# Joint attention with values as weights: four heads' exponentials as one streamed operand, normalised on GpSimd

## What is computed

```
kv_in = concatenate([context_hidden, draft_hidden], axis=1)
k, v = kv_in @ Wk.T, kv_in @ Wv.T          # 4 heads each, repeated for 4 query heads
scores = einsum('bhqd,bhkd->bhqk', q, k) * SCALE
probs = softmax(scores, axis=-1)
attn = einsum('bhqk,bhkd->bhqd', probs, v)
return attn @ Wo.T                          # added to x, then the next layer norm
```

## Time and profile before

| | us |
|---|---|
| three runs | 2807.26, 2809.73, 2812.78 (median 2809.73) |
| profiled execution, span from first to last instruction | 2808.8 |
| stage `joint4` within it | about 1883 to 2275 |

### The profile page before, as it was taken

One profiled execution on the slowest core, in us unless ns is written; L12 is line 12 of the kernel. 1 busy time (PEld: TensorE's weight loads), 2 busy tenths in 40 slices (PEclk: granted clock), 3 DMA queues, 4 the chain that ended last, 5 costly groups with the idle time before them and its releaser, 6 DMA issues. The chain is left out here.

```text
span 2808.8 us, 49906 instructions
## 1 busy us (share of the span) xinstructions
PE 2598.3 (93%) x15563; PEld 2142.5 (76%) x15564; DVE 1717.6 (61%) x3341; ACT 1129.9 (40%) x2434; POOL 764.2 (27%) x791
## 2 busy tenths in 40 slices
PE   8999799979899999799996998989999999899998
PEld 7888677768688777578875876767777788788887
DVE  4537767669777666576665576864444435656564
ACT  2103255523343324455543233755444421444343
POOL 3213100024333235423233101740000012345455
PEclk9999999999899979899997998999999989999999
DMA  5454122125622045477773432353212031666664
GB/s 191 152 144 99 36 87 73 45 73 162 175 73 63 17 145 188 141 216 219 197 225 86 127 71 75 117 174 91 87 49 87 8 129 58 164 158 150 159 150 82
DMA packets 289285, 332.98 MB, mean 119 GB/s; under 512 B 147446, under 2 KB 202694, under 8 KB 287313
## 3 DMA queue, kind: packets, MB, share of 16 engines
q1 hardware_dynamic: 217904, 252.57, 28.8%
q0 software_dynamic: 20640, 51.74, 9.3%
q10 hardware_dynamic: 50560, 26.34, 3.2%
HBM read 233.86 MB, written 96.72 MB: 118 GB/s over the span
## 5 line engine op out<-in xcount | busy, mean ns | idle before, releaser
L898 PE MATMUL e_psum<-e_up_hi,hT_hi 128*128 x672 | 246.8, 367 | 21.3 <-DVE hT_lo L867 12.7
L900 PE MATMUL e_psum<-e_up_hi,hT_lo 128*128 x672 | 238.1, 354 | 0.0
L899 PE MATMUL e_psum<-e_up_lo,hT_hi 128*128 x672 | 238.0, 354 | 0.0
L898 PEld LDWEIGHTS e_psum<-e_up_hi,hT_hi 128*128 128x128 f32 x672 | 128.7, 192 | 43.8 <-issue 32.4
L1565 POOL TENSOR_TENSOR self_a_p<-self_a_p,self_a_mx 112x448 f32<-112x448 f32 x96 | 96.0, 1000 | 205.2 <-DVE self_a_mx L1622 205.2
L794 ACT ACTIVATE e_gate<-e_psum 128x352 f32<-128x352 f32 (+1 forms) x86 | 44.4, 516 | 260.1 <-PE e_psum L900 256.0
L873 DVE TENSOR_TENSOR hT_lo<-e_psum,hT_hi 128x256 fp32r<-128x256 f32 (+2 forms) x138 | 55.7, 435 | 143.4 <-ACT hT_hi L812 135.6
L1656 ACT ACTIVATE self_a_p<-self_a_p 112x448 f32<-112x448 f32 x128 | 71.6, 575 | 165.0 <-POOL self_a_p L1565 113.9
L900 PEld LDWEIGHTS e_psum<-e_up_hi,hT_lo 128*128 128x128 f32 x672 | 128.6, 191 | 11.7
L899 PEld LDWEIGHTS e_psum<-e_up_lo,hT_hi 128*128 128x128 f32 x672 | 128.8, 192 | 9.9
L1786 PEld LDWEIGHTS joint_psum<-x_v,joint_a_pt 125*112 125x112 f32 (+1 forms) x1024 | 120.1, 179 | 19.8 <-issue 14.4
(11 more groups left out here) (563 smaller groups left out, 7385.1 us busy)
## 6 DMA issues: line engine op xcount, KB each, us to landing
e_up_raw<-in_L_ffn_w SPq DMA_DIRECT2D x64, 512.0 KB, 4.9
e_up_raw<-in_L_ffn_w SPq DMA_DIRECT2D x64, 352.0 KB
e_dn_raw<-in_L_ffn_w SPq DMA_DIRECT2D x16, 1024.0 KB, 15.0
q_all<-p_p_t_stage ACTq DMA_DIRECT2D x56, 256.0 KB
e_dn_raw<-in_L_ffn_w SPq DMA_DIRECT2D x16, 512.0 KB
x_q<-q_all SPq DMA_DIRECT2D x8, 896.0 KB
v_ctx<-front_c_v_stage SPq DMA_DIRECT2D x24, 250.0 KB
x_others<-k_ctx SPq DMA_DIRECT2D x8, 750.0 KB, 4.7
```

Of the source, the lines that this page charges most:

```text
L898: pe.matmul(out, lhs[0], rhs[0], start=k == 0, stop=False)
L899: pe.matmul(out, lhs[0], rhs[1], start=False, stop=False)
L900: return pe.matmul(out, lhs[1], rhs[0], start=False, stop=k == n_k - 1)
```

## The change

The stage gets an attention part of its own, `JointAttentionPart`. Its scores, maxima, exponentials and transposes are those of before. What differs:
- The reciprocal of the row sums comes per step (two heads), on VectorE behind this step's maxima, for the heads of the step before (L1973).
- GpSimd multiplies the exponentials (112 x 487, in place) by it (L1920), one instruction per head, and TensorE's transposes wait for `p_ready` in place of `exp_done`.
- The copies write four heads side by side, and each chunk of the values is the weight (L1953): per group of four heads, which share one key and value head, four products over 448 columns instead of sixteen over 128. The result has features on partitions, which is what the output projection needs.
- VectorE's evacuation and the four transposes of the output part are gone. "o" reads its high and low halves from the values' bank; `o_used`, the low half's semaphore, frees that bank for the next group.

The diff, cut (the other two attention parts only get `turned = False`):

```diff
+class JointAttentionPart:
...
+        def gpsimd(pool):
...
+            for step in range(n_all + LE):
+                for i in items(step, 1):
+                    r = i % RING
+                    pool.wait_ge(rinv_ready, i // W + 1)
+                    pool.tensor_tensor(p[:, r, :], p[:, r, :], rinv[:, r:r + 1].to_broadcast([T, S]), ALU.mult).then_inc(p_ready, 1)
+                yield
+                yield
...
+        def tensor(pe):
...
+            for step in range(n_all + LE):
+                for t in items(step, LT):
+                    pe.wait_ge(p_ready, t + 1)
+                    reuse(pe, pt_ready, t - N_T + 1)
+                    for c in range(nch):
...
+                        last = pe.transpose(ps[0:n, t_banks[t % N_T], c * T:(c + 1) * T], p[:, t % RING, offs[c]:offs[c] + n],
+                                            core.ident[0:T, 0:T])
+                    last.then_inc(t_done, 1)
+                for i in items(step):
...
+                    reuse(pe, exp_done, i - N_S + 1)
+                    pe.matmul(ps[0:T, s_banks[i % N_S], 0:S], q[:, b % 2, h, :],
+                              k[:, b % 2, h // group, :], start=True, stop=True).then_inc(s_done, 1)
+                yield
+                gr = closed(step, LP, group // W)
+                if gr is not None:
...
+                    pe.wait_ge(pt_ready, (gr + 1) * group)
+                    reuse(pe, self.o_used, gr)
+                    for c in range(nch):
+                        n = key_chunks[c]
+                        last = pe.matmul(ps[:, o_bank, 0:group * T], v[0:n, b % 2, c, j * dh:(j + 1) * dh],
+                                         pt[0:n, gr % 2, c, :, :].rearrange("p h t -> p (h t)"), start=(c == 0), stop=(c == nch - 1))
+                    last.then_inc(pv_done, 1)
+                yield
...
+        def vector(dve):
...
+                before = items(step, 1)
+                if before:
+                    r = before[0] % RING
+                    dve.wait_ge(exp_done, before[-1] + 1)
+                    dve.reciprocal(rinv[:, r:r + W], rsum[:, r:r + W]).then_inc(rinv_ready, 1)
+                yield
+                yield
...
+        def scalar(act):
...
+                    to = pt[:, t // group % 2, :, t % group, :]
...
 class OutNormPart:
...
+        self.ht_ready, attention.o_used = ht_ready, (lo_ready if turned_in else oq_ready if quantise_in else t_done)
...
-                    act.wait_ge(t_done, i + 1)
+                    act.wait_ge(ot_done, i + 1)
...
-                    act.activation(oT_hi[:, i % OT_RING, :, :], t_view, ACT.Copy).then_inc(hi_ready, 1)
+                    act.activation(oT_hi[:, i % OT_RING, :, :], ot_view(i), ACT.Copy).then_inc(hi_ready, 1)
...
-                    if shift <= at < shift + n_g:
+                    if shift <= at < shift + n_g and not turned_in:
...
-                a = CrossAttentionPart(g, "a", 128, lambda b: q_all[:, tokens_of(b)],
+                a = JointAttentionPart(g, "a", lambda b: q_all[:, tokens_of(b)],
...
-                                       [CT] * CCH + [T], 128.0 ** -0.5, (0, 1, 2), (3, 4), (5,), 2, tiles=(q4, k4, v4))
+                                       [CT] * CCH + [T], 128.0 ** -0.5, (0, 1, 2), (3, 4), 5, (q4, k4, v4))
```

More of the change, by code:

```diff
@@ L1497, in __init__ @@
         self.o = o = g.sb(f"{name}_o", [T, O_RING, 512])
-        self.evacs_per_group, self.o_ring = per_group, O_RING
+        self.evacs_per_group, self.o_ring, self.turned = per_group, O_RING, False
         qk_in, v_in = g.sems(f"{name}_qk_in", 2), g.sems(f"{name}_v_in", 2)
@@ L1680, in __init__ @@
         n_all = B * n_steps
-        self.steps, self.lead, self.evacs_per_group, self.o_ring = 2 + 2 * (n_all + LE), 2 * LE, per_unit // per_bank, O_RING
+        self.steps, self.lead, self.evacs_per_group, self.o_ring, self.turned = 2 + 2 * (n_all + LE), 2 * LE, per_unit // per_bank, O_RING, False
         loaded = tiles is not None
@@ L1888, in __init__ @@
         core, ps, x = g.core, g.ps, g.core.x
-        o, n_o = attention.o, attention.o_ring
+        turned_in = attention.turned
+        o, n_o = (None, 0) if turned_in else (attention.o, attention.o_ring)
         n_g = n_k // 4
@@ L1917, in __init__ @@
         rows_out = g.sems(f"{name}_rows_out", 2)
-        self.ht_ready, attention.o_used = ht_ready, (oq_ready if quantise_in else t_done)
+        self.ht_ready, attention.o_used = ht_ready, (lo_ready if turned_in else oq_ready if quantise_in else t_done)
         o_split = hi_ready if quantise_in else lo_ready
+        ot_done = attention.ot_done if turned_in else t_done
         T_BANK, Y_BANK = banks
         t_view = ps[:, T_BANK, 0:4 * T].rearrange("p (c t) -> p c t", c=4)
+        ot_view = attention.ot_view if turned_in else lambda i: t_view
         two_norms = norm == "ln_rms"
@@ L2021, in phase @@
                     dve.wait_ge(hi_ready, i + 1)
-                    dve.tensor_tensor(oT_lo[:, i % OT_RING, :, :], t_view, oT_hi[:, i % OT_RING, :, :].bitcast(F32),
+                    dve.tensor_tensor(oT_lo[:, i % OT_RING, :, :], ot_view(i), oT_hi[:, i % OT_RING, :, :].bitcast(F32),
                                       ALU.subtract).then_inc(lo_ready, 1)
@@ L2081, in tensor @@
                         weights_ready(pe, i)
+                        if i == 0 and free is not None and turned_in:
+                            free(pe)
                         pe.wait_ge(o_split, i + 1)
@@ L2096, in tensor @@
                         placed = min(B * n_g, ((b * stride + TURN - shift) // stride) * n_g + min(n_g, (b * stride + TURN - shift) % stride + 1))
-                        pe.wait_ge(o_split, placed)
+                        if not turned_in:
+                            pe.wait_ge(o_split, placed)
                         reuse(pe, ht_ready, b)
```

94 lines of the change are left out of this document (added).

## The result

The changed kernel takes **2819.26 us** (median; 2814.17 to 2820.82) against 2808.70 (2805.87 to 2812.78): a ratio of 1.0028, 95% interval [1.0018, 1.0039], or 8 us slower by the interval's middle and 10.6 by the medians. It is slower, as forecast; the forecast of 2835 was 16 us too high, so it had the loss more than twice too large.

The account below looks back on a forecast made before the run. TensorE's own work was taken to bound the joint stage, a new loop through GpSimd replacing it: +5.5 in the batches, +10.5 clock, +9 start, sum +25 us, 2834 as span, 2835 us as median; range 2808 to 2861.

Parts of the forecast that it names:

- The loop that I drew: Joint stage: scores, maxima, reciprocal, two GpSimd multiplications, transposes, next scores form a loop with its own length, 5.6 us.
- one of the signs that I had named for being right: Joint stage: TensorE waits for GpSimd's products ahead of most transposes, for 3 us once per batch.
- L = 5.6 us: Loop's length from start of scores to next scores, summed from rows; floor for each two-head step, giving 47.65 per batch.
- The term of +5.5: Steps 8 to 63, seven batches: 47.65 us per batch by the loop's floor against 46.87 before, +5.5 us.
- L = 5.46: Loop length below which the rival that TensorE stays the bound was to decide; that rival: 2785 us, 10%.
- lower bound of 5.44: Loop length with GpSimd at 0.93 us an operation; steps come out even, 2814 us, within a rival of 17%.
- 1.5 for each of seven empty steps: +10.5: Steps with nothing behind their scores: TensorE's wait drops its clock, slowing transposes and scores by 1.5 us each, +10.5 us.
- The loop without the clock: Rival: the clock stays up in every empty step; +5.5 and +5 for the start, 2820 us; 17%.
- Start: +9: Stage's first eight steps: 50 us instead of 42, plus 1 us for weight splits meeting multiplications, +9 us.
- At the end O fills the waits: 0: Stage's end: output projection blocks fill TensorE's waits, costing 0.
- The next V waits for that split … hidden by T and S: nothing.: Values wait for the output part's split to free their only bank; transposes and scores hide it, cost nothing.
- TensorE's work of 43.5 per batch: Joint stage: cheaper values and dropped output transposes cut TensorE's work per batch to 43.5 us.

Follow-up runs that it names:

- early: Changed kernel with the reciprocal of the previous step's sums placed ahead of the step's two row maxima on VectorE: 2789.58 us.
- double: Changed kernel with a second, wasted multiplication per head on GpSimd into a spare tile ahead of the real one: 2944.24 us (one run).
- dve: Changed kernel with the two multiplications on VectorE right behind the reciprocal, instead of on GpSimd: 2796.85 us.
- normonly: Kernel before with only GpSimd's multiplication ahead of the transposes and a plain copy as evacuation, values in their old form: 2851.93 us.
- fill: Changed kernel with twelve wasted products of 512 columns on TensorE in the step with nothing behind its scores: 2809.26 us.
- fill4: Changed kernel with four wasted products on TensorE in the step with nothing behind its scores: 2818.80 us.
- half: Changed kernel with GpSimd multiplying only the first 243 of 487 exponentials per head, so another output: 2789.36 us, total not comparable.
- normearly: Kernel of "normonly" with the reciprocal ahead of the two maxima on VectorE: 2806.88 us.
- fill8: Changed kernel with eight wasted products on TensorE in the step with nothing behind its scores: 2808.25 us (one run).

## Why the prediction was right in direction and wrong in size

- **The mechanism was right, its reach was not.** The loop that I drew exists: "early", "double", "dve" and "normonly" moved the time by changing its length or its order alone. But it sets only three of a batch's eight steps, the empty one and two with output blocks; the others go by TensorE's own work. So one of the signs that I had named for being right, transposes that wait for GpSimd ahead of most steps, didn't come: the long waits are one per batch.
- **"L = 5.6 us" is the step that failed.** Measured from scores to scores it is 5.37 (2052.96 to 2058.33 in a step with an output block). I set the reciprocal's end at +2.90 with a gap behind the negation; it overlaps the negation and ends at +2.76. The products took 1.95 for my 1.98, and waking with the second head's transposes took 0.58 for my 0.62. Small as they are, they decide: at 5.37 a step with values (5.48, TensorE's own work) isn't held at all. In "fill" a batch is four steps with values of 5.48, two of 5.36 (the empty one and one with an output block), one of 5.58 (the other output block) and one of 8.44 (two output blocks and N), from scores to scores: 46.67 instead of my 47.65. The 5.58 is a step that I had missed: in the kernel after, GpSimd's pair takes 2.17 there instead of 1.95. It starts at 2078.81, while VectorE scales the tokens for the norm (L2215, 0.53 us from 2078.65); that this overlap is what stretches it wasn't tested. The term of +5.5 is in truth −0.2 × 6 = −1.2, the largest miss of the sum. The prediction's own point of decision, L = 5.46 (5.47 by its formula), lay within the error of a sum of eight rounded rows, so the forecast belonged on both sides of it. Its lower bound of 5.44 is 5.47 by its own rows, on that same point.
- **"1.5 for each of seven empty steps: +10.5"** was right in kind and a little large. In the kernel after the six full batches have a low each, in the mean for 48.0 − 46.67 = 1.33 us: +8.0. The seventh empty step, in the last stretch, has the same wait of 2.09 us (until 2259.24) and none: its window above shows 1.00. Where batches with and without a low stand side by side ("fill4", "half") it costs 1.7; against 46.67, the six of the change cost 1.67, 1.52, 1.31, 1.22, 1.14 and 1.18. All last about 3.4 us, but by windows of 0.4 us they begin 1.2, 0.7, 0.3 and 0.1 us behind the end of the wait, and in the last two batches right at it. The first batch's transposes, to be read beside the eight from 2067.70 above:

```profile
1971.17 0.68 PE L1933 MATMUL joint_psum<-ident,joint_a_p 112*125 112x112 f32 x4 [2.09 <-POOL joint_a_p L1920]
...
1972.13 0.94 PE L1933 MATMUL joint_psum<-ident,joint_a_p 112*125 112x112 f32 x4 [0.28 <-POOL joint_a_p L1920]
```

In the first batch the first head's four run at the full clock, and TensorE then stands for 0.28 more until the second product is there; from the third batch on most or all of their time is at the low clock, and that second wait is gone. So an early low falls in part on time that would have been idle, and costs less. "The loop without the clock" named nearly the right total, 2820, from the wrong terms: luck.

- **"Start: +9" was +3.8.** Scores of step 2 came 11.0 us in (estimated 10), and those of step 8 at 47.7 instead of 41.7, so 6.0 of loss; the rest of the way to the first addition has no empty step and took 2.2 less. I stopped my count at step 8.
- **"At the end O fills the waits: 0"** was +1.5.
- **"The next V waits for that split … hidden by T and S: nothing."** True of the change, where the loop is longer; false once it is gone ("early": 0.9 per batch).
- **TensorE's work of 43.5 per batch** held: 44.44 − 0.90 in "early" is 43.5.
- **"A multiplication takes 1.01 us"** held (0.99 to 1.00), but for the one longer pair per batch named above. The Trainium skill ("GPSIMD Engine Reference", Elementwise — side-by-side cycle accounting) would have given 1.07 for 487 elements (an estimate from its 4497 ns for 2048); the trace is 7% better.
- **"1 us for the few" splits that meet a multiplication** was nothing; the last section has the rows.
- **Behind the stage**, 4.3 us of the loss are missing. The profile of the kernel before has two lows there, one of 3.4 us at 0.53 and one from 2655.9 to 2659.4 at 0.61, that no other profile of a kernel with the same output has at these places. At 1.7 us each, an estimate from "fill4", they are 3.4 of the 4.3. With them this stretch takes 538.7; the change and the nine others take 530.9 to 535.2 ("normearly", whose code there is that of the kernel before, 533.3). So I don't count it to the change; whether the kernel before has these lows in every execution isn't known, since only one was profiled.

The sum by measured terms is −1.2 + 8.0 + 3.8 + 1.5 = 12.1, the stage's 12.1. It closes by construction, since the price of the lows is a difference of two periods; what tests it is that "fill4" and "half" show the low's price within one run.

## What to carry to other kernels

An operation put on an idle engine is free only if what releases it comes early: look first at what stands ahead of its releaser on the in-order engine between, and move that before judging the operation. Here the same multiplications cost 28 us of the stage or nothing by the place of one reciprocal of 0.15 us. And where a forecast rests on a loop against a block of work, and the two differ by less than the error of their rows, give both sides their chance.

## What the runs showed of the hardware

**More work, less time.** Where an idle stretch lets TensorE's clock fall, wasted products in it gave back 8.2 us of the stage ("fill").

**The length of a wait doesn't tell whether the clock falls.** In seven empty steps per kernel, at the same place: waits of 2.1 us (the change) were followed by a low in six of seven, of 1.7 ("half") in four, of 1.5 ("dve") in none, of 1.2 ("fill4") in five, of 0.3 ("fill8") in none. Batches of the same kernel ("half") thus take 45.4 or 47.1 us. What decides between them isn't settled here.

**A split of weights beside a multiplication.** In the start of the kernel after (order of time):

```profile
1889.52 1.23 DVE L2031 TENSOR_TENSOR joint_wo_lo<-joint_w_raw,joint_wo_hi 128x1024 fp32r<-128x1024 f32 x1 [2.42 <-ACT joint_wo_hi L2023]
1894.03 1.42 DVE L2031 TENSOR_TENSOR joint_wo_lo<-joint_w_raw,joint_wo_hi 128x1024 fp32r<-128x1024 f32 x1 [1.70 <-ACT joint_wo_hi L2023]
```

```profile
1892.42 1.95 POOL L1920 TENSOR_TENSOR joint_a_p<-joint_a_p,joint_a_rinv 112x487 f32<-112x487 f32 x2 [7.41 <-DVE joint_a_rinv L1973]
```

The split that began 0.34 us before GpSimd's pair ended took 0.19 longer than the free one, while the pair took its usual 1.95; four of the six splits up to 1920 did so. In the earlier trace rows it was GpSimd, the later one there, that was stopped. So the meetings cost VectorE 4 × 0.19 = 0.8 us and TensorE nothing: VectorE stood idle behind each of these four splits for 1.0 to 1.8 us, until the next scores were there.
